# A fused attention and mixture-of-experts layer: the second expert's weight preparation placed behind the last attention output, and the router softmax of the last but one sequence placed at the end of the last sequence's steps

## The chip, the cores and the metric

One core of a Trainium2 chip runs one program. The metric is the device time of the whole program in microseconds (us); lower is better. The engines are PE (TensorE, matmuls), DVE (VectorE), ACT (ScalarE), POOL (GpSimd) and SP (SyncE, which here only starts transfers). Each engine works through its own list of instructions strictly in the order in which the program issues them; engines wait for one another by semaphores.

## What is computed

The input is `x` of 8 sequences, 512 tokens, 256 channels, in float32. The reference, cut to what matters:

```python
k, q, v = proj(W_key), proj(W_query), proj(W_value)      # 16 heads of 16
scores = where(causal, q k^T / sqrt(16), -inf)
out = softmax(scores) v, heads joined, times W_proj^T / 16
x = layernorm(x + out)

s = softmax(x router_w^T, over 8 experts)                # per token
gate_vals, sel_idx = top_k(s transposed, 129)            # per sequence and expert
tokens = x[sel_idx]
y = gelu(tokens @ w1[e] + b1[e]) @ w2[e] + b2[e]         # 256 -> 1024 -> 256
out = zeros.at[sel_idx].add(y * gate_vals)
x = layernorm(x + out)
```

## The kernel before, in words

The kernel has two parts. `attention` (lines 225 to 892) does everything up to the first layernorm, the router's scores and the choice of tokens for the first six sequences. `experts` (lines 1024 to 1453) does the expert layers, the choice for the last two sequences and the second layernorm. In each part every engine has a function that walks through one common list of stages and issues what concerns it.

**The list of attention.** `steps()` (lines 120 to 170) writes this list out. It walks over an index `i`, and for each `i` over 40 places, `place = 10 * g + k`. At a place it yields one score block of sequence `i` (`st`), and the stages that the table `STAGES` (lines 52 to 87) puts at `(g, k)`, each with an offset `ahead` that says which sequence it works on: at index `i` the table's output projection, `rstd`, `logit`, `lexp`, `x1` and `score` stages belong to sequence `i - 1`. There is one more index, `i = B` (8), which only holds the tail of sequence 7. A pair in the code such as `(B, 12)` is an index and a place.

**The stages that matter here.** All line numbers are those of the profile.

- `st`: PE makes a block of scores (L784), ACT takes its exponential (L539), POOL masks it (L468). Two banks `st_ps` are shared in turn, so PE waits for ACT after two blocks.
- `av`: PE multiplies the exponentials by the values (L816), ACT copies the result (L564). `onorm`: PE transposes it (L825), DVE divides (L685, L689). `ot`: PE transposes back (L868), ACT copies (L596). `proj`: four output tiles by PE (L877), and for each of them three DVE instructions (L694, L696, L699); after the fourth DVE writes the variance (L704, L707). The fourth `proj` of sequence 7, at `(B, 21)`, is the last output of attention.
- `rstd`: POOL makes the reciprocal deviation (L497 to L499). `logit`: DVE makes the router's logits (L618, L621, L623). `lexp`: ACT takes the exponential of the logits (L527) and so has to wait for L623. `score`: DVE makes the shares of the softmax (L627, L628, L629) and has to wait for L527. `x1`: ACT finishes a tile of rows (L521); SP stores the rows (L371).
- `pick`, `round`, `picked`, `joined`, `fetch`: the choice of tokens for sequences 0 to 5. DVE runs 17 rounds, each of a maximum of eight, its indices and a replacement (L181, L182, L184); they stand at places 11 to 37 of index 7 (`ROUND_AT`, line 109). After the last one DVE writes `best_f` (L727). At `(B, 3)` PE transposes the result (L207), DVE copies it (L729, L730), PE mirrors one half (L889), DVE joins the halves (L737 to L753), and POOL gathers the tokens of the first two jobs (L513). All `av` blocks of the last group of heads stand behind this on PE, at `(B, 4)` to `(B, 7)`.
- `cut` and `low`: every expert weight is split into a rounded high part and a low part, the rest. The high part is a copy by ACT into the type fp32r; the low part is a subtraction. For expert 0 this is `cut 0` (ACT L553, POOL L505) inside index 7. For expert 1, `load` at `(B - 1, 39)` makes SP fetch both weights (L427, L429); `cut 1` is two copies by ACT of 128x2048 each (L558), for `w1` at `(B, 1)` and for `w2` at `(B, 12)`; `low` at `(B, 11)` is four subtractions by DVE of 128x512 each (L714), for `w1` alone. Those of `w2` belong to `experts` (L1316).

**The start of experts.** The list there is `expert_steps()` (lines 964 to 1005). It begins with `turn` of job 0 and `lastlog`:

```python
yield "turn", 0, 0
yield "lastlog", 0, 0
```

`turn` has PE transpose the gathered tokens (L1389), ACT copy the high part (L1217) and DVE subtract for the low part (L1273). `lastlog` is the `logit`, `lexp` and `score` of sequence 7. Then come the `up` stages: PE (L1416) begins the first one only when both parts of the tokens are there,

```python
if n == 0:
    pe.wait_ge(tp_hi, KC * (q + 1))
    pe.wait_ge(tp_lo, KC * (q + 1))
    pe.wait_ge(w1_cut, PIECES * (e + 1))
```

and ACT then applies Gelu (L1226), for which it loads another table, and copies the high part (L1231); POOL (jobs 0 and 1) subtracts (L1187). `down` (L1434) multiplies by `w2`. SP loads `w1` of expert 2 (L1120) once the low part of expert 1's `w1` is done.

Of the kernel before, what the change touches and what calls it, by code (L numbers as in the profile page):

```python
# [15 lines left out]
B, T, C = 8, 512, 256  # L16
# [87 lines left out]
ROUNDS = -(-CAP // 8)  # L104
PIECES = 4
CUT_AT = [(B - 1, 12 + 3 * piece) for piece in range(2 * PIECES)]
NEXT_CUT_AT, NEXT_LOW_AT = ((B, 1), (B, 12)), (B, 11)
PICK_AT = ((B - 2, 33), (B - 2, 35), (B, 3))
ROUND_AT = [(B - 1, place) for place in (11, 12, 14, 15, 17, 18, 20, 21, 23, 24, 26, 27, 29, 31, 33, 35, 37)]

# [9 lines left out]
def steps():  # L120

    for i in range(-3, B + 1):
        for g in range(4):
            nat_b, nat_0 = (4 * i + g + NAT_LEAD) // 4, (4 * i + g + NAT_LEAD) % 4 * N_QUARTER
            for k in range(10):
                if (i, g, k) == (-1, 3, 0):
                    yield "nmcut", 0, 0
                    yield "v", 1, 2
                    yield "v", 1, 3
                    yield "nm", 0, 0  # L130
                if 0 <= i < B:
                    yield "st", i, (2 * g) * UP + k
                if 0 <= nat_b < B:
                    for n in range(N_QUARTER * k // 10, N_QUARTER * (k + 1) // 10):
                        yield "nat", nat_b, nat_0 + n
                group = i * GROUPS + g - 1
                if k in AV_PLACES and 0 <= group < B * GROUPS:
                    yield "av", group, AV_PLACES.index(k)
                if (i, g, k) == (-2, 0, 0):
                    for stage, n in (("qk", 0), ("qk", 1), ("stack", 0), ("centre", 0), ("qk", 2), ("qk", 3), ("v", 0), ("v", 1), ("v", 2), ("v", 3)):  # L140
                        yield stage, 0, n
                if (i, g, k) == (-1, 2, 0):
                    yield "fold", 0, 0
                for gg, kk, stage, ahead, n in STAGES:
                    if (gg, kk) == (g, k) and 0 <= i + ahead < B and (i, stage, n) not in STARTED:
                        yield stage, i + ahead, n
                for gg, kk, stage, n in SECOND_AT:
                    if i == -1 and (gg, kk) == (g, k):
                        yield stage, 1, n
                        if (stage, n) == ("qk", 1):  # L150
                            yield "stack", 1, 0
                place = 10 * g + k
                if (i, place) == PICK_AT[0]:
                    yield "halved", 0, 0
                if (i, place) == PICK_AT[1]:
                    yield "pick", 0, 0
                if (i, place) in ROUND_AT:
                    yield "round", 0, ROUND_AT.index((i, place))
                if (i, place) in CUT_AT:
                    yield "cut", 0, CUT_AT.index((i, place))  # L160
                if (i, place) == (B - 1, 39):
                    yield "load", 1, 0
                if (i, place) in NEXT_CUT_AT:
                    yield "cut", 1, NEXT_CUT_AT.index((i, place))
                if (i, place) == NEXT_LOW_AT:
                    yield "low", 1, 0
                if (i, place) == PICK_AT[2]:
                    yield "picked", 0, 0
                    yield "joined", 0, 0
                    yield "fetch", 0, 0  # L170


def numbers(stages):

    return {x: n for n, x in enumerate(x for x in steps() if x[0] in stages)}
# [49 lines left out]
def attention(nc, block, both, ctx, xt_d, x_d, wqkv_d, wp_d, wpn_d, rw_d, x1_d, acc_d, ident, mirror, halves, scores, chosen, w1_d, w2_d, b1_d, ahead):  # L225
# [127 lines left out]


    banked = [x for x in steps() if x[0] in BY_ACT + BY_DVE]
    turn_no = {x: n for n, x in enumerate(banked)}

# [9 lines left out]
    def _(sp):  # L367
# [12 lines left out]
        load_xt(0)  # L380
        sp.dma_start(rw[:, :, :], rw_d.rearrange("(k p) n -> p k n", p=P)).then_inc(rw_in, 16)
        for stage, b, n in steps():
            if stage == "split" and b + 1 < B:
                sp.wait_ge(x_split, b + 1)
# [1140 lines left out]
```

## Time and profile before

| what | value |
|---|---|
| time, three runs | 892.38, 891.51, 891.24 us; median 891.51 us |
| profiled execution | 894.26 us, of which the span of all instructions 892.5 us |
| PE busy | 821.0 us, 92% of the span |
| DVE busy | 606.6 us, 68% |
| ACT busy | 532.7 us, 60% |
| POOL busy | 468.0 us, 52% |
| mean granted clock of PE | 0.979 |
| share of the last chain | PE 72%, DVE 14%, ACT 6% |

All times of rows are counted from the start of the span. A timeline row gives the start, the duration, the engine, the line, the operation and the tiles, and in brackets how long the engine stood idle before it and which instruction ended that wait. A row with "x4" merges four instructions in a row. "issue" as a releaser means that the profile shows no instruction that the engine waited for. A granted clock of 1.00 is 2.4 GHz, one of 0.50 is 1.2 GHz. Attention ends and the experts begin at about 460 us.

### The profile page before, as it was taken

The page shows a single profiled execution, that of the slowest core. Times are in us where ns is not written, and L with a number is a line of the kernel's source. Part 1 is how long each engine was busy: PE and PEld are TensorE (multiplying, and loading weights), DVE is VectorE, ACT ScalarE, POOL GpSimd, SP SyncE. Part 2 cuts the span into 40 slices and gives each one's busy share as a digit, 9 for nine tenths or more (in the row PEclk, how much of TensorE's full clock was granted, in tenths as well). Part 3 has the DMA queues.
Part 4 walks back from the last instruction along what each step waited for, and adds up shares of the span by engine and source line. Part 5 has one row for each costly group of instructions (what it writes and reads, how often), then busy time and mean ns, then how long its engine had stood idle before and what let it go on. Part 6 is the DMA issues. An engine that isn't in the chain of part 4 may idle for free.

```text
span 892.5 us, 17252 instructions
## 1 busy us (share of the span) xinstructions
PE 821.0 (92%) x5908; PEld 615.5 (69%) x5908; DVE 606.6 (68%) x2067; ACT 532.7 (60%) x1048; POOL 468.0 (52%) x640
## 2 busy tenths in 40 slices
PE   4779999999999999998778999999999999999994
PEld 3534454454645454433258999999999999999993
DVE  5668777788788778899858854546464554646466
ACT  2247767667586766666647445555565656555546
POOL 6458565666655565344658356445444444545343
PEclk9779999999999999999899999999999999999998
DMA  4863434536352424610253223335243342613275
GB/s 144 221 191 112 133 107 151 155 107 185 123 149 95 159 91 156 192 64 11 89 199 109 30 44 60 91 83 145 40 103 69 53 129 40 150 28 52 31 208 188
DMA packets 89574, 100.12 MB, mean 112 GB/s; under 512 B 8592, under 2 KB 82960, under 8 KB 89360
## 3 DMA queue, kind: packets, MB, share of 16 engines
q1 hardware_dynamic: 72128, 77.66, 27.8%
q0 software_dynamic: 12368, 16.52, 11.4%
q10 hardware_dynamic: 4992, 4.85, 1.8%
q8 instruction: 47, 0.77, 0.4%
q14 instruction: 39, 0.32, 0.1%
HBM read 65.38 MB, written 33.23 MB: 110 GB/s over the span
## 4 chain that ended last, share of the span: by engine, by line
PE 72%; DVE 14%; ACT 6%; issue 3%; POOL 1%; DMA 1%; SPq 1%; ACTq 1%; DVEq 0%; POOLq 0%
PE y_ps L1434 22%; PE h_ps L1416 18%; PE av_ps L816 7%; PE st_ps L784 5%; DVE n_ps L648 5%; PE n_ps L799 5%; PE stage_ps L835 3%; PE stage_ps L877 3%; PE stage_ps L843 3%; PE tp_ps L1389 2%; ACT pt L539 1%; DVE nmax L648 1%; DVE best_at L182 1%; DVE row_pool L184 1%; DVE nm L680 1%
## 5 line engine op out<-in xcount | busy, mean ns | idle before, releaser
L648 DVE CUSTOM_DVE_ANT_0 n_ps<-n_ps,tri 128x512 f32<-128x512 f32 (+3 forms) x512 | 238.6, 519 | 72.5 <-PE n_ps L799 70.5
L539 ACT ACTIVATE pt<-st_ps 128x512 f32<-128x512 f32 x320 | 184.4, 602 | 60.5 <-PE st_ps L784 45.5
L1434 PE MATMUL y_ps<-w_parts,h_hi 128*128 128x256 f32 (+1 forms) x1152 | 215.8, 281 | 2.0 <-POOL h_lo L1187 1.6
L1226 ACT ACTIVATE g<-h_ps,b 128x384 f32<-128x384 f32 (+1 forms) x192 | 104.1, 542 | 164.8 <-PE h_ps L1416 138.4
L1434 PEld LDWEIGHTS y_ps<-w_parts,h_hi 128*128 128x128 f32 (+1 forms) x1152 | 172.6, 177 | 5.9 <-issue 1.9
L1416 PE MATMUL h_ps<-tt_hi,w_parts 128*128 128x384 f32 (+1 forms) x768 | 169.7, 323 | 3.7 <-issue 2.0
L1198 POOL DMA_INDIRECT acc<-y,tok_no x61 | 98.1, 1608 | 140.7 <-DVE y L1342 132.7
L1326 DVE TENSOR_TENSOR h_lo<-g,h_hi 128x384 fp32r<-128x384 f32 (+1 forms) x176 | 90.1, 513 | 115.4 <-ACT h_hi L1231 95.6
L468 POOL TENSOR_SCALAR_AFFINE_SELECT pt<-pt 128x256 f32<-128x256 f32 (+1 forms) x320 | 109.8, 361 | 105.4 <-ACT pt L539 104.6
L1434 PE MATMUL y_ps<-w_parts,h_lo 128*128 128x256 f32 (+1 forms) x576 | 161.5, 280 | 0.0
L784 PE MATMUL st_ps<-w_parts 99*128 99x512 bf16 (+3 forms) x512 | 125.7, 307 | 17.5 <-ACT pt L539 15.9
L799 PE MATMUL n_ps<-w_parts 96*128 96x512 bf16 (+3 forms) x512 | 124.1, 307 | 7.4 <-DVE nmax L648 5.0
L1416 PEld LDWEIGHTS h_ps<-tt_hi,w_parts 128*128 128x128 f32 x768 | 125.4, 188 | 4.7 <-issue 2.2
L1434 PEld LDWEIGHTS y_ps<-w_parts,h_lo 128*128 128x128 f32 (+1 forms) x576 | 102.0, 177 | 2.1
L784 PEld LDWEIGHTS st_ps<-w_parts 99*128 99x128 bf16 x512 | 41.6, 98 | 88.6 <-ACT pt L539 60.5
L1231 ACT ACTIVATE h_hi<-g 128x384 fp32r<-128x384 f32 (+1 forms) x192 | 94.4, 492 | 7.4
L816 PE MATMUL av_ps<-pt,vaug 128*32 128x512 f32 (+3 forms) x1024 | 95.6, 447 | 0.0
L1416 PE MATMUL h_ps<-tt_lo,w_parts 128*128 128x384 f32 (+1 forms) x384 | 91.3, 319 | 0.0
L1169 POOL DMA_INDIRECT tok<-x,tok_no x58 | 57.9, 999 | 33.9 <-issue 33.9
L648 DVE DVE_READ_ACCUMULATOR2_ANT nmax<- 128x1 f32 x512 | 72.3, 141 | 0.0
L799 PEld LDWEIGHTS n_ps<-w_parts 96*128 96x128 bf16 x512 | 43.9, 98 | 36.5 <-DVE nmax L648 22.7
L1416 PEld LDWEIGHTS h_ps<-tt_lo,w_parts 128*128 128x128 f32 x384 | 66.2, 188 | 0.0
(209 smaller groups left out, 1091.0 us busy)
## 6 DMA issues: line engine op xcount, KB each, us to landing
w_parts<-part_d SPq DMA_DIRECT2D x186, 128.0 KB, 2.8
w_raw<-in_w SPq DMA_DIRECT2D x16, 1024.0 KB
part_d<-w_raw SPq DMA_DIRECT2D x96, 128.0 KB, 2.2
w_raw<-in_xt SPq DMA_DIRECT2D x8, 512.0 KB, 4.2
res<-in_x SPq DMA_DIRECT2D x8, 512.0 KB, 4.7
x<-res SPq DMA_DIRECT2D x8, 512.0 KB, 3.3
acc<-res SPq DMA_DIRECT2D x8, 512.0 KB, 5.1
fin<-acc SPq DMA_DIRECT2D x4, 512.0 KB, 4.5
```

The source lines that it names most:

```text
L468: nc.gpsimd.affine_select(out=x, in_=x, compare_op=ALU.is_ge, fill=0.0, base=0, pattern=[[0, len(tiles)], [1, P]], channel_multiplier=-1). ...
L539: nc.scalar.activation(pt[:, slot % PT_RING, n % UP, :], st_ps[at % ST_RING][:, :], ACT.Exp, scale=S_SCALE).then_inc(exp_done, 1)
L648: ins = nc.vector.tensor_tensor_reduce(out=src[:, h, :], in0=src[:, h, :], in1=mask, scale=-1.0, scalar=-BIG_NEG, op0=ALU.add, op1=ALU.min ...
L784: ins = nc.tensor.matmul(st_ps[at % ST_RING][:, c:c + T - kb * P], kst[0:KM, b % 2, h, kb * P:(kb + 1) * P], qst[0:KM, b % 2, h, kb * P:T] ...
L799: ins = nc.tensor.matmul(bank[:, j * w:(j + 1) * w], qst[0:KQ, b % 2, h, qb * P:(qb + 1) * P], kst[0:KQ, b % 2, h, 0:w], start=True, stop= ...
L816: ins = nc.tensor.matmul(av_ps[VW * j:VW * (j + 1), n * P:T], vaug[:, seq % 3, n, h, :], pt[:, (seq * PAIRS + h // 2) % PT_RING, u, c:c + ...
L1198: nc.gpsimd.indirect_dma_start(acc_d[0:reach(j), :], bass.IndirectOffsetOnAxis(ap=choice(e, j), axis=0), y[0:rows_of(j), j, :], None, comp ...
L1226: nc.scalar.activation(g[:, at % G_RING, 0:cols], h_ps[at % H_RING][:, 0:cols], ACT.Gelu, bias=b1[:, e, n:n + 1]).then_inc(g_done, 1)
L1231: nc.scalar.activation(h_hi[:, q % 2, n, 0:cols], g[:, at % G_RING, 0:cols], ACT.Copy).then_inc(g_hi, 1)
L1326: nc.vector.tensor_tensor(h_lo[:, q % 2, n, 0:cols], g[:, at % G_RING, 0:cols], h_hi[:, q % 2, n, 0:cols].bitcast(F32), ALU.subtract).then ...
L1416: ins = nc.tensor.matmul(h_ps[at % H_RING][:, 0:cols], w[e % 2][:, k, units], x[:, q % TOK_RING, k, 0:cols], start=i == 0, stop=i == len(t ...
L1434: ins = nc.tensor.matmul(y_ps[at % Y_RING][0:rows, 0:C], x[:, q % 2, m, toks], w[e % 2][:, m, :], start=i == 0, stop=i == len(terms) - 1)
```

## The change

Three stages move in the list of attention; nothing is added or taken away. The two copies (L558) go from `(B, 1)` and `(B, 12)` to `(B, 24)` and `(B, 25)`, and the four subtractions (L714) from `(B, 11)` to `(B, 26)`, behind the last `proj` and `rstd` of sequence 7. At index 7 alone, that is for sequence 6, `lexp` goes from place 29 to place 38, and `score` from place 32 to place 39.

```diff
@@ -104,7 +104,8 @@
 ROUNDS = -(-CAP // 8)
 PIECES = 4
 CUT_AT = [(B - 1, 12 + 3 * piece) for piece in range(2 * PIECES)]
-NEXT_CUT_AT, NEXT_LOW_AT = ((B, 1), (B, 12)), (B, 11)
+NEXT_CUT_AT, NEXT_LOW_AT = ((B, 24), (B, 25)), (B, 26)
+SCORE_AT = {'lexp': (3, 8), 'score': (3, 9)}
 PICK_AT = ((B - 2, 33), (B - 2, 35), (B, 3))
 ROUND_AT = [(B - 1, place) for place in (11, 12, 14, 15, 17, 18, 20, 21, 23, 24, 26, 27, 29, 31, 33, 35, 37)]
 
@@ -142,6 +143,8 @@
                 if (i, g, k) == (-1, 2, 0):
                     yield "fold", 0, 0
                 for gg, kk, stage, ahead, n in STAGES:
+                    if i == B - 1:
+                        gg, kk = SCORE_AT.get(stage, (gg, kk))
                     if (gg, kk) == (g, k) and 0 <= i + ahead < B and (i, stage, n) not in STARTED:
                         yield stage, i + ahead, n
                 for gg, kk, stage, n in SECOND_AT:
```

## Rows read from the trace of the kernel before

**Rows 1.** Timeline of ACT and PE around the router's exponential of sequence 6.
```profile
431.38 1.08 ACT L539 ACTIVATE pt<-st_ps 128x512 f32<-128x512 f32 x2
435.17 0.23 ACT L527 ACTIVATE lge<-lg 128x32 f32<-128x32 f32 x1 [2.70 <-DVE lg L623]
...
436.42 0.61 PE L784 MATMUL st_ps<-w_parts 99*128 99x256 bf16 x2 [3.51 <-ACT pt L539]
```

**Rows 2.** Groups of DVE from 413.03 to 445.05 us: count, busy us, mean ns, idle.
```profile
L182 DVE FIND_INDEX8 best_at<-best,row_pool 112x8 uint32<-112x256 f32 x17 | 7.1, 419 | 0.0
```

**Rows 3.** Timeline of DVE: shares, what follows them, end of the rounds, next wait.
```profile
439.59 0.19 DVE L627 TENSOR_REDUCE lsum<-lge 128x4 f32<-128x32 f32 x1
...
440.13 0.25 DVE L685 RECIPROCAL rden<-stage_ps 128x16 f32<-128x16 f32 x1
...
444.77 0.27 DVE L727 CAST best_f<-best_at 112x136 f32<-112x136 uint32 x1
446.18 0.42 DVE L729 COPY sides<-stage_ps 128x256 f32<-128x256 f32 x1 [1.14 <-PE stage_ps L207]
```

**Rows 4.** Timeline of PE: the first transpose of the choice, the last outputs.
```profile
445.19 0.29 PE L207 MATMUL stage_ps<-ident,best_f 112*128 112x112 f32 x1 [0.26 <-DVE best_f L727]
...
454.73 5.50 PE L877 MATMUL stage_ps<-wp,o_t 128*128 128x264 f32 x16 [0.83 <-ACT o_t L596]
```

**Rows 5.** Timeline of ACT from its first weight copy to the experts' first tokens.
```profile
447.88 1.91 ACT L558 ACTIVATE w_parts<-w_raw 128x2048 fp32r<-128x2048 f32 x1 [1.93 <-issue]
450.39 0.60 ACT L564 ACTIVATE av_sb<-av_ps 128x512 f32<-128x512 f32 x1 [0.60 <-PE av_ps L816]
450.89 1.90 ACT L558 ACTIVATE w_parts<-w_raw 128x2048 fp32r<-128x2048 f32 x1
453.50 1.08 ACT L596 ACTIVATE o_t<-stage_ps 128x512 f32<-128x512 f32 x2 [0.71 <-PE stage_ps L868]
460.60 0.87 ACT L1217 ACTIVATE tt_hi<-tp_ps 128x384 fp32r<-128x384 f32 x2 [6.01 <-PE tp_ps L1389]
```

**Rows 6.** Timeline of DVE: the four subtractions and what follows them.
```profile
452.61 2.53 DVE L714 TENSOR_TENSOR w_parts<-w_raw,w_parts 128x512 fp32r<-128x512 f32 x4
456.71 0.42 DVE L694 SCALAR_TENSOR_TENSOR res<-stage_ps,res 128x256 f32<-128x256 f32 x1 [1.57 <-PE stage_ps L877]
```

**Rows 7.** Timelines of DVE, POOL, PE and ACT where the experts begin.
```profile
461.70 0.17 DVE L707 TENSOR_SCALAR ve<-mv 128x4 f32<-128x4 f32 x1
461.78 1.01 DVE L1273 TENSOR_TENSOR tt_lo<-tp_ps,tt_hi 128x384 fp32r<-128x384 f32 x2
...
463.66 0.19 DVE L623 TENSOR_TENSOR lg<-lg,rstd 128x32 f32<-128x32 f32 x1 [0.55 <-POOL shift L499]
...
461.96 1.04 POOL L497 TENSOR_TENSOR rstd<-ve,half 128x4 f32<-128x4 f32 x1 [5.35 <-DVE ve L707]
...
460.07 0.82 PE L1389 MATMUL tp_ps<-ident,tok 128*128 128x128 f32 x6
462.90 0.58 PE L1416 MATMUL h_ps<-tt_hi,w_parts 128*128 128x384 f32 x2 [2.01 <-issue]
...
464.26 1.28 ACT L1226 ACT_TABLE_LOAD   x1
465.55 0.58 ACT L1226 ACTIVATE g<-h_ps,b 128x384 f32<-128x384 f32 x1
```

**Rows 8.** Timeline of PE: end of the first unit, a wait, first `down`.
```profile
463.67 0.86 PE L1416 MATMUL h_ps<-tt_hi,w_parts 128*128 128x384 f32 x4
...
473.02 0.62 PE L1416 MATMUL h_ps<-tt_hi,w_parts 128*128 128x384 f32 x2 [1.67 <-ACT g L1226]
...
479.09 0.36 PE L1434 MATMUL y_ps<-w_parts,h_hi 128*128 128x256 f32 x1 [1.60 <-POOL h_lo L1187]
```

**Rows 9.** Windows: length, busy us (count) of PE, PEld, DVE, ACT, POOL, granted clock, DMA.
```profile
435.00:440.00 5.00, 2.69 (x13) 1.53 (x17) 4.64 (x18) 4.83 (x11) 2.41 (x5) 0.50 0.00 0
440.00:445.00 5.00, 4.92 (x40) 1.00 (x32) 4.67 (x17) 3.12 (x7) 2.90 (x6) 0.87 0.93 298
...
455.00:460.00 5.00, 5.00 (x16) 3.81 (x16) 2.47 (x10) 0.00 (x0) 1.30 (x2) 0.67 0.25 72
460.00:465.00 5.00, 2.99 (x20) 2.71 (x18) 3.91 (x19) 1.85 (x4) 2.70 (x7) 1.00 0.70 249
```

**Rows 10.** Weight subtractions of DVE by line: shortest, middle and longest ns, starts.
```profile
L714 DVE TENSOR_TENSOR w_parts<-w_raw,w_parts x4: 682/684/725, 452.6 to 454.4; 128x512 fp32r<-128x512 f32 x4
L1316 DVE TENSOR_TENSOR w_parts<-w_raw,w_parts x4: 693/1328/1509, 471.0 to 475.6; 128x512 fp32r<-128x512 f32 x4
```

## The prediction

> **What bounds the kernel now.** I read the page first: PE has 92% of the span, so what counts is where PE stands still, and the change touches only the stretch from about 430 to 480 us. There I read the timelines engine by engine, then the windows for the clock.
>
> The first thing to see is the stall that the moved exponential makes. ACT ends a pair of score exponentials at 432.46, then stands idle for 2.70 us until DVE's logits let the router's exponential run at 435.17, and PE, behind it, stands idle for 3.51 us [rows 1]. It looks like a prize of about 3 us. But DVE in the same stretch never stops: 17 rounds of the choice, with zero idle before their index searches, run from 413.03 to 445.05 [rows 2], and what comes next on PE, the transpose of the choice, waited only for DVE's `best_f` (0.26 us, at 445.19) [rows 3, 4]. So up to 445 DVE is the bound, and an earlier PE only waits longer there.
>
> The second thing is the tail from 445 to 460. It is one chain of short steps through PE, ACT and DVE. The weight preparation stands beside it: the first copy ends at 449.79 and ACT still waits 0.60 us for PE; the second ends at 452.79 and ACT waits 0.71 us [rows 5]. The four subtractions end at 455.14 and DVE then waits 1.57 us for the first output [rows 6]. All six instructions are covered; taking them from here gives nothing.
>
> The third is the start of the experts. DVE goes from the variance (L707) straight to the low part of the tokens (461.78 to 462.79), and PE starts `up` at 462.90, right after it. DVE's logits of sequence 7 wait 0.55 us for POOL and start L623 at 463.66; the exponential, the table load at 464.26 and the first Gelu at 465.55 hang on it [rows 7]. From there to the first `down` at 479.09 ACT and POOL set the pace (PE waits for Gelu and for POOL's subtraction [rows 8]); behind it PE is busy without a break, so what is late at 479 is late at the end.
>
> **The change part by part.**
>
> *Router exponential and shares, sequence 6.* ACT no longer waits at 432.46 and runs up to 435.30 - 432.46 = 2.8 us ahead (435.30 is about when it resumes, L527 taking 0.23 us from 435.17, with overlap) [rows 1]. The row tiles and their store by SP, the two weight loads behind it on SP, and expert 0's last weight pieces on POOL all come as much earlier; none is waited for by the chain. On DVE the shares leave the chain of rounds: 439.59 to 440.13, 0.54 us, so `best_f` comes 0.54 us sooner [rows 3]. Behind the rounds they fall into DVE's idle 1.14 us before L729 [rows 3], which covers them; without that cover they would cost the 0.54 again. PE ended its scores 0.26 us before L207, so it is ready. Gain on the chain: 0.54 us.
>
> *The two copies on ACT.* 1.91 + 1.90 = 3.81 us, now behind the `ot` copies that end at 454.58. ACT is idle for 6.01 us from there until the experts' tokens at 460.60 [rows 5]. They end near 458.4: covered, with 2.2 us to spare. The loads are long there, since the second copy already ran at 450.89. Cost 0.
>
> *The four subtractions on DVE.* They go into the DVE queue between L707 and L1273. Nothing covers them: DVE has no idle there [rows 7]. Behind them wait `tt_lo` and so PE's first `up`, and the logits and so ACT's exponential, table load and Gelu. By the row they take 2.53 us [rows 6]. Lower bound 2.53. Upper bound: the same kind of subtraction took up to 1.51 us instead of 0.69 beside POOL's subtractions [rows 10]; here POOL has one long instruction beside it, the 1.04 us power of `rstd` [rows 7], so at most 1.04 us more. I take 0.5, half of it, since the nearest rows show both.
>
> The Trainium skill (SBUF — State Buffer, Who interferes with whom) says that a DVE instruction with two SBUF inputs and a GpSimd instruction that reads SBUF exclude one another for a whole instruction. By that rule the term would be the whole 1.04 us; by the L714 row alone it would be nothing. `tt_lo`, which ran beside the power without loss, reads one operand from PSUM.
>
> *From DVE to the Gelu.* `tt_lo` and PE's `up` come 2.53 - 0.54 = 1.99 us later. The logits had waited 0.55 us for POOL, which will be done long before. So the exponential and the Gelu come 1.99 - 0.55 = 1.44 us later without contention, 1.94 with it. SP's load of expert 2's `w1` comes as much later and is needed only jobs later. The four row tiles of sequence 7 and POOL's gathers shift along.
>
> *PE's clock.* Before, PE stood idle 2.01 us between the token transposes and `up` and kept a granted clock of 1.00 [rows 7, 9]. Now that gap is 2.01 + 2.53 to 3.03, about 4.8 us. The nearest row is the 3.51 us of idle: behind it the clock was 0.50 from 435 to 440 and, by the 0.87, until 441.3, some 4.8 us after PE resumed at 436.42; the other dip, 455 to 458.3 (0.67 x 5 us), came after scattered short transposes [rows 9]. So I expect half clock for 3.3 to 4.8 us of `up`. At half clock PE loses half that time, 1.7 to 2.4 us. PE leads ACT there: the first unit's last matmuls are in the four that start at 463.67, so it is done by about 464.2, and Gelu started at 465.55 [rows 7, 8], a lead of 1.3 us, which shrinks by 1.99 - 1.44 to 0.8. So ACT is late by 0.9 to 1.6 us more; I take 1.2. Lower bound 0 (clock stays up), upper 2.4 (no lead left).
>
> *Sum.* -0.54 + 2.53 - 0.55 + 0.5 + 1.2 = +3.14, about +3.1 us. It is a difference within the profiled execution (894.26 us, span 892.5 and 1.8 around it), which stands 2.75 us above the median of the three runs. I apply it to the median: 891.5 + 3.1 = 894.6 us.
>
> **The rivals.**
>
> 1. *The plain sum.* The clock holds over the gap and POOL does not get in the way: +1.44 us, 892.9. For it: the 2.01 us gap cost nothing. Against: a gap of more than twice that, and the 3.51 us one was punished.
>
> 2. *The clock also falls in the tail.* With the stall gone PE finishes its scores up to 3 us before `best_f`, and until the last `av` it then has only transposes. Half clock over `av`, transposes and outputs would add to the chain; the 16 output matmuls took 5.50 us with 3.3 us of dip [rows 4, 9], that is about 1.7 us lost per such dip. +3.1 + 1.7 = +4.8, 896.3. Against it: the clock might recover before `av`.
>
> 3. *The clock is better placed in the tail.* PE has no 3.5 us hole at 433, and the dip over the outputs goes away: 1.7 us less on PE, of which DVE's own three instructions per tile leave about 1.0. +1.44 - 1.0 = +0.4, 891.9.
>
> 4. *Faster: the first copy was in the way in the timed runs.* ACT waited 1.93 us for something that the profile does not name, which I read as the landing of expert 1's `w1`; the copy ended 0.60 us before PE's result [rows 5]. If the load lands over 0.60 us later in an unprofiled run, the copy delays ACT's L564, and with it the whole tail; the change takes that away. With a landing 3 us later it would give 2.4 us; with the better clock as well, 1.44 - 2.4 - 1.0 = -2.0, 889.5. It decides against the rest when the landing is more than about 2 us later. The trace has the landing in time, and the three runs lie within 1.2 us, so this is weak.
>
> 5. *The score move does nothing*, if ACT had another wait in the same place: then 0.54 is missing and the result is +3.7, inside the forecast's range.
>
> **How the numbers follow.** Forecast (+2.4 to +4.2, with or without part of contention and clock) 0.50; rival 1, 0.17; rival 2, 0.14; rival 3, 0.09; rival 4, 0.06; others 0.04. A measurement of this kernel tells about 0.2%, 1.8 us, from no change. Slower by more than that: the forecast and rival 2, and the fifth of rival 1 whose contention lifts it over 893.3: 0.67. Within: rest of rival 1, rival 3 and some others, 0.25. Faster: rival 4 and a rest, 0.08. The range leaves out rival 4 and the ends of rival 2: from 891.8, below rival 3, to 897.0, which is rival 2 with the full contention of 1.04 instead of 0.5.
>
> **What would show it.** In the changed profile: L527 for sequence 6 behind the last scores, no 2.7 us idle on ACT at 432; PE waiting up to 3 us for `best_f` before L207; `best_f` near 444.5; the copies between the `ot` copies and L1217; the four L714 directly behind L707, near 461.3 to 464; `up` starting near 465 to 465.4; the first Gelu near 467 to 467.5; the granted clock at 0.50 for part of 464 to 470; the first `down` near 482.3. I am wrong if PE's first `up` is less than 1 us later than 462.90, or if the time is below 891.8: then either the subtractions found cover or the tail gained more than the rounds' 0.54 us.

## The result, and the profile after

The changed kernel takes 897.0 us (median of 6 runs, 895.67 to 900.07) against 891.56 us for the kernel before in the same comparison; the ratio is 1.0064 with a 95% interval of 1.0052 to 1.0077, that is 4.6 to 6.9 us slower. The ratios leave out two executions in a much slower state, one of the kernel before (1307.58 us) and one of `subs_only` below (1562.88 us). The direction was forecast, the size was not: +3.1 us, with a range up to 897.0. The profiled execution is the slowest of the six (900.07 us), as that of the kernel before also stands above its median (894.26 us); its span is 898.3 us against 892.5, so +5.8 us is the difference to be found. Line numbers from 107 on are 1 to 3 higher than before: L816 is now L819, L877 is L880, L1416 is L1419.

PE of the changed kernel, timeline:

```profile
433.38 0.61 PE L787 MATMUL st_ps<-w_parts 99*128 99x256 bf16 x2 [0.58 <-ACT pt L542]
...
445.56 0.29 PE L210 MATMUL stage_ps<-ident,best_f 112*128 112x112 f32 x1 [2.92 <-DVE best_f L730]
...
448.03 4.50 PE L819 MATMUL av_ps<-pt,vaug 128*32 128x512 f32 x32
...
457.19 5.42 PE L880 MATMUL stage_ps<-wp,o_t 128*128 128x264 f32 x16 [0.83 <-ACT o_t L599]
...
467.67 0.98 PE L1419 MATMUL h_ps<-tt_hi,w_parts 128*128 128x384 f32 x2 [4.41 <-issue]
...
484.86 0.36 PE L1437 MATMUL y_ps<-w_parts,h_hi 128*128 128x256 f32 x1 [1.55 <-POOL h_lo L1190]
```

The stall of 3.51 us [rows 1] is gone (0.58 us at 433.38), and PE waits for `best_f` instead, 2.92 us where it had waited 0.26 [rows 4]. Then comes what I had only as a rival: the last `av` block takes 4.50 us. In the kernel before the same 32 matmuls read:

```profile
447.37 2.36 PE L816 MATMUL av_ps<-pt,vaug 128*32 128x512 f32 x32
```

Two DVE rows of the kernel before, to compare with (L621 and L1273 are L624 and L1276 now):

```profile
434.72 0.19 DVE L621 TENSOR_TENSOR lg<-scores,lmax 128x32 f32<-128x32 f32 x1
...
468.13 1.02 DVE L1273 TENSOR_TENSOR tt_lo<-tp_ps,tt_hi 128x384 fp32r<-128x384 f32 x2 [3.04 <-issue]
```

DVE and POOL of the changed kernel, timelines:

```profile
434.59 1.14 DVE L624 TENSOR_TENSOR lg<-scores,lmax 128x32 f32<-128x32 f32 x1
435.76 0.32 DVE L626 TENSOR_TENSOR lg<-lg,rstd 128x32 f32<-128x32 f32 x1
...
445.19 0.23 DVE L730 CAST best_f<-best_at 112x136 f32<-112x136 uint32 x1
...
464.07 0.17 DVE L710 TENSOR_SCALAR ve<-mv 128x4 f32<-128x4 f32 x1
464.15 2.49 DVE L717 TENSOR_TENSOR w_parts<-w_raw,w_parts 128x512 fp32r<-128x512 f32 x4
466.56 1.01 DVE L1276 TENSOR_TENSOR tt_lo<-tp_ps,tt_hi 128x384 fp32r<-128x384 f32 x2
...
434.41 1.26 POOL L508 TENSOR_TENSOR w_parts<-w_raw,w_parts 128x512 fp32r<-128x512 f32 x1 [0.33 <-ACT w_parts L556]
...
464.33 1.41 POOL L500 TENSOR_TENSOR rstd<-ve,half 128x4 f32<-128x4 f32 x1 [7.17 <-DVE ve L710]
```

`best_f` starts 0.42 us later than before (444.77 [rows 3]), not 0.54 us earlier. The reason is L624, a logit subtraction of 128x32, which took 0.19 us before and takes 1.14 here; it starts 0.18 us after a POOL subtraction and ends 0.06 us after that one ends. L626 behind it takes 0.32 us instead of 0.19, so the two cost 1.08 us more; less the 0.54 us of the shares that makes 0.54, of which 0.12 don't show in the 0.42, because the whole stretch lies 0.12 us earlier in this profile (the PE block at 432.04 before starts at 431.92). The four subtractions of the weights cost what their row said, 2.49 us.

ACT of the changed kernel, timeline:

```profile
468.15 0.23 ACT L530 ACTIVATE lge<-lg 128x32 f32<-128x32 f32 x1 [4.31 <-DVE lg L626]
470.01 1.28 ACT L1229 ACT_TABLE_LOAD   x1 [1.63 <-PE h_ps L1419]
471.31 0.58 ACT L1229 ACTIVATE g<-h_ps,b 128x384 f32<-128x384 f32 x1
```

The table load now waits 1.63 us for PE's first unit of `up`. Before, it came 0.14 us behind the exponential's end and 1.36 us behind the start of `up` [rows 7].

Windows of the changed kernel (the third number from the end is the granted clock):

```profile
435.00:440.00 5.00, 5.00 (x24) 1.57 (x23) 4.71 (x15) 3.37 (x7) 3.45 (x7) 0.51 0.55 184
440.00:445.00 5.00, 2.63 (x27) 0.75 (x23) 4.67 (x17) 2.77 (x6) 1.67 (x5) 1.00 1.01 309
445.00:450.00 5.00, 3.60 (x22) 1.78 (x26) 3.21 (x18) 0.00 (x0) 0.33 (x1) 0.68 0.40 136
450.00:455.00 5.00, 4.08 (x32) 2.05 (x24) 1.39 (x5) 0.60 (x1) 3.78 (x5) 0.64 0.28 79
455.00:460.00 5.00, 3.88 (x15) 3.08 (x16) 0.82 (x4) 4.04 (x4) 1.85 (x2) 0.70 0.29 82
460.00:465.00 5.00, 3.26 (x17) 2.47 (x15) 4.17 (x17) 1.51 (x3) 0.67 (x1) 0.96 0.24 66
465.00:470.00 5.00, 2.33 (x7) 2.36 (x8) 3.96 (x13) 0.23 (x1) 4.06 (x9) 0.73 0.79 279
```

The clock is down four times: from 435 to 440, over the `av` block, over the outputs and over the first unit of `up`. The first and the third are there before as well [rows 9]. The first is there although the stall of 3.51 us ahead of it is gone.

How late each landmark is, after minus before, from these rows and those of before:

| landmark | before | after | late by |
|---|---|---|---|
| `best_f` starts | 444.77 | 445.19 | 0.42 |
| last `av` block starts | 447.37 | 448.03 | 0.66 |
| outputs start | 454.73 | 457.19 | 2.46 |
| variance | 461.70 | 464.07 | 2.37 |
| first `up` | 462.90 | 467.67 | 4.77 |
| first Gelu | 465.55 | 471.31 | 5.76 |
| first `down` | 479.09 | 484.86 | 5.77 |

The span's 5.8 us is complete at the first `down`: about 2.4 us before the variance, 2.4 us of subtractions, 1.0 us between `up` and Gelu. One part of this comparison stays open: from the end of the `av` block to the first output it is 5.00 us in the profile before, 4.66 in this one and 4.23 to 4.26 in all twelve others of the study. No run tells why.

### The profile page after: what moved, and what is told of

Same layout as the page of the kernel before. It is cut to its first block, busy times and chain, and to the rows that moved or that the text cites. A ratio compares the mean times of both kernels' runs of the same rounds, so it can differ in the third digit from the quotient of the medians.

```text
span 898.3 us, 17251 instructions
## 1 busy us (share of the span) xinstructions
PE 827.3 (92%) x5908; PEld 620.5 (69%) x5908; DVE 605.6 (67%) x2067; ACT 532.3 (59%) x1048; POOL 468.8 (52%) x640
## 4 chain that ended last, share of the span: by engine, by line
PE 72%; DVE 14%; ACT 6%; issue 3%; POOL 2%; DMA 2%; ACTq 1%; SPq 0%; DVEq 0%; POOLq 0%
PE y_ps L1437 22%; PE h_ps L1419 18%; PE av_ps L819 7%; PE st_ps L787 5%; PE n_ps L802 5%; DVE n_ps L651 5%; PE stage_ps L838 4%; PE stage_ps L846 3%; PE stage_ps L880 3%; PE tp_ps L1392 2%; ACT pt L542 1%; DVE nmax L651 1%; DVE best_at L185 1%; DVE row_pool L187 1%; PE stage_ps L871 1%
## 5 line engine op out<-in xcount | busy, mean ns | idle before, releaser
L1419 PE MATMUL h_ps<-tt_hi,w_parts 128*128 128x384 f32 (+1 forms) x768 | 170.8, 324 | 5.7 <-issue 4.4
L1419 PEld LDWEIGHTS h_ps<-tt_hi,w_parts 128*128 128x128 f32 x768 | 126.2, 189 | 6.7 <-issue 4.6
L819 PE MATMUL av_ps<-pt,vaug 128*32 128x512 f32 (+3 forms) x1024 | 98.2, 459 | 0.0
L1419 PE MATMUL h_ps<-tt_lo,w_parts 128*128 128x384 f32 (+1 forms) x384 | 91.8, 320 | 0.0
L1419 PEld LDWEIGHTS h_ps<-tt_lo,w_parts 128*128 128x128 f32 x384 | 66.8, 189 | 0.0
```

Of the source, the lines that this page charges most:

```text
L819: ins = nc.tensor.matmul(av_ps[VW * j:VW * (j + 1), n * P:T], vaug[:, seq % 3, n, h, :], pt[:, (seq * PAIRS + h // 2) % PT_RING, u, c:c + ...
L1419: ins = nc.tensor.matmul(h_ps[at % H_RING][:, 0:cols], w[e % 2][:, k, units], x[:, q % TOK_RING, k, 0:cols], start=i == 0, stop=i == len(t ...
```

## The experiments

### The parts apart

Four kernels in one comparison, each timed against the kernel before (median 891.86).

**score_only**: `lexp` and `score` moved, weight work at its old places.

```diff
-NEXT_CUT_AT, NEXT_LOW_AT = ((B, 24), (B, 25)), (B, 26)
+NEXT_CUT_AT, NEXT_LOW_AT = ((B, 1), (B, 12)), (B, 11)
```

> Only the router's exponential and shares of sequence 6 are moved; the weight copies and subtractions stay where they were before. Theory A (the score move costs by PE's clock and by one blocked DVE instruction): in the profile after, the choice's last rounds ended 0.4 us later, not 0.54 us earlier, since the logits' L624 ran 1.14 us beside a POOL subtraction, and the last av block took 4.50 us at half clock instead of 2.36; together the first output matmul came 2.5 us later. So this kernel alone should be about 2 to 2.5 us slower than before, near 893.8, and its granted clock between 447 and 453 us should be at 0.50. Rival B (my prediction: the score move gains 0.54 us and all the loss is in the weight subtractions): 891.0, best_f ending near 444.5.

Measured: 894.31 us, ratio 1.0026 (1.0018 to 1.0035), so 2.3 us slower. Its DVE and PE timelines:

```profile
433.55 1.14 DVE L624 TENSOR_TENSOR lg<-scores,lmax 128x32 f32<-128x32 f32 x1
...
444.52 0.42 PE L210 MATMUL stage_ps<-ident,best_f 112*128 112x112 f32 x1 [2.45 <-DVE best_f L730]
...
447.75 3.55 PE L819 MATMUL av_ps<-pt,vaug 128*32 128x512 f32 x32
```

Both marks are there: L624 at 1.14 us and a slow `av` block. The move that I had booked as a gain is a loss.

**weights_only**: copies and subtractions moved, router stages at their old places (`SCORE_AT = {}`).

> Only the two copies and the four subtractions are moved; the router's exponential and shares stay. Theory A: the four subtractions put 2.5 us between the variance and the tokens' low part, PE's first up starts 2.5 us later (near 465.4), and it may come back at half clock, up to 1 us more on the first Gelu: +2.5 to +3.5 us, 894.0 to 895.0. Av block at about 2.4 us. Rival B (the parts only hurt together): within 1 us of before.

Measured: 895.27 us, ratio 1.0037 (1.0024 to 1.0050), 3.3 us slower.

```profile
447.92 2.36 PE L819 MATMUL av_ps<-pt,vaug 128*32 128x512 f32 x32
...
463.40 0.58 PE L1419 MATMUL h_ps<-tt_hi,w_parts 128*128 128x384 f32 x2 [4.41 <-issue]
...
465.20 1.28 ACT L1229 ACT_TABLE_LOAD   x1 [1.09 <-PE h_ps L1419]
```

The `av` block is at full speed, and the gap ahead of `up` is 4.41 us instead of 2.01. The two parts add: 2.3 + 3.3 = 5.6 us, the whole change 5.7 by its ratio. The prediction's terms for this part were 2.53 - 0.55 + 0.5 + 1.2 = 3.7 us.

**subs_only**: as weights_only, but the copies stay at `(B, 1)` and `(B, 12)`.

> Only the four DVE subtractions are moved behind the last output; the two ACT copies stay at their old places and the router's stages too. Theory A: the copies are free in both places, so this is the same as weights_only within 0.4 us (894.0 to 895.0). Rival B: the copies behind the ot copies cost something of their own (ACT busy 3.7 us ahead of the experts' tokens), then this is faster than weights_only by 1 us or more.

Measured: 894.98 us, ratio 1.0030 (1.0018 to 1.0041). The intervals of the two overlap widely: no cost or gain of the copies is seen in either place, as forecast.

**subs_after_logits**: as weights_only, with the subtractions issued behind the logits and shares of sequence 7 (the stage `low` of attention is left out).

```diff
                 for ins in take_halves(nc, halves, scores, slice(EARLY, B)):
                     ins.then_inc(halved, 1)
+                dve.wait_ge(w1_top, 2 * PIECES)
+                for piece in range(PIECES):
+                    nc.vector.tensor_tensor(piece_of(w1_lo[1], "w1", piece), piece_of(w1_raw, "w1", piece),
+                                            piece_of(w1_hi[1], "w1", piece).bitcast(F32), ALU.subtract).then_inc(w1_cut, 1)
```

> As weights_only, but the four subtractions are issued in the experts' part behind the logits, shares and halves of sequence 7, where DVE stood idle 3.04 us before the second job's tokens. Theory A (what costs is only the place in front of the tokens' low part and the logits): the 2.5 us disappear into that idle time, up starts near 462.9 and the time is 891.5 within 0.6. Rival B (the work on DVE is what costs, wherever it stands in the experts' part): 893.5 to 894.5. Rival C: the subtractions now run beside POOL's subtractions, take 1.1 to 1.5 us each instead of 0.6 and push the second job's tokens: +1 to +2.

Measured: 891.57 us, ratio 0.9993 (0.9984 to 1.0001), no difference from before. Its DVE timeline:

```profile
462.68 2.49 DVE L1280 TENSOR_TENSOR w_parts<-w_raw,w_parts 128x512 fp32r<-128x512 f32 x4
465.81 1.02 DVE L1270 TENSOR_TENSOR tt_lo<-tp_ps,tt_hi 128x384 fp32r<-128x384 f32 x2 [0.65 <-ACT tt_hi L1214]
```

The same 2.49 us, a few instructions later, fill what was DVE's wait of 3.04 us for the second job's tokens, and 0.65 us of it is left.

### What makes the score move a loss

**after_tail_fill**: the changed kernel with idle PE time filled ahead of `best_f`.

```diff
             elif stage == "picked":
+                for _ in range(12):
+                    nc.tensor.matmul(ps[:, :], ident_b[:, :], tri[:, :, :].rearrange("p a k -> p (a k)"), start=True, stop=True)
                 pe.wait_ge(best_ready, 1)
```

> The changed kernel with 12 extra matmuls of 128x512 bf16 on PE, issued before it waits for best_f, into the bank that the transposes then overwrite; their results are not used. Theory A (the lower clock over the last av block comes from PE standing idle ahead of best_f): the idle 2.9 us is filled, the clock stays at 1.00 from 446 to 453, the av block takes 2.36 us instead of 4.50, and the time falls by 1.5 to 2 us against the changed kernel, to about 895.2. Rival B (the clock falls whatever PE does there, or what counts is the tail's short steps): av still 3.5 to 4.5 us and 897.0.

Measured: 895.94 us, ratio 1.0041 (1.0029 to 1.0054), about 1.1 us less than the changed kernel by the medians, 2.1 by the ratios; the two intervals just touch, so the size is uncertain.

```profile
443.17 2.75 PE L888 MATMUL stage_ps<-tri,ident_b 128*128 128x512 bf16 x12
...
447.92 2.36 PE L819 MATMUL av_ps<-pt,vaug 128*32 128x512 f32 x32
```

Nothing but PE's idle time was changed, and the `av` block is back at 2.36 us. Over all 14 profiles of the study the block took 2.36 us in the four with the router stages at their old place, 3.55 to 4.50 in the five that move them, and 2.36 in the five that move them and have the extra matmuls. In the five with the longer block PE had stood idle for 2.27 to 3.26 us ahead of `best_f`, in the nine others for 0.53 us at most.

**score_cut6**: score_only with expert 0's last two weight pieces later.

```diff
-CUT_AT = [(B - 1, 12 + 3 * piece) for piece in range(2 * PIECES)]
+CUT_AT = [(B - 1, at) for at in (12, 15, 18, 21, 24, 27, 32, 34)]
```

> As score_only, but expert 0's seventh weight piece (ACT copy and POOL subtraction) stands at place 32 instead of 30, and the eighth at 34, so that POOL isn't subtracting when DVE makes the logits of sequence 6. Theory A (L624's 1.14 us is a wait for POOL's 1.27 us subtraction, as both read two SBUF operands): L624 takes 0.19 us again and best_f ends 0.95 us earlier relative to the rounds before it; the time falls by about 1 us against score_only, to 893.3. Rival B (the 1.14 us belong to the order of DVE's own work): L624 stays at 1.14 us.

Measured: 892.23 us, ratio 1.0002 (0.9993 to 1.0011). DVE, POOL and PE timelines:

```profile
434.47 0.23 DVE L624 TENSOR_TENSOR lg<-scores,lmax 128x32 f32<-128x32 f32 x1
...
444.03 0.23 DVE L730 CAST best_f<-best_at 112x136 f32<-112x136 uint32 x1
...
436.25 1.27 POOL L508 TENSOR_TENSOR w_parts<-w_raw,w_parts 128x512 fp32r<-128x512 f32 x1 [0.61 <-ACT w_parts L556]
...
446.73 3.86 PE L819 MATMUL av_ps<-pt,vaug 128*32 128x512 f32 x32
```

With POOL's subtraction at 436.25 instead of beside it, L624 takes 0.23 us, and `best_f` starts 0.74 us earlier than before; measured from the score blocks at 432.04 (here 431.80) it is 0.50, the forecast 0.54 us. The time fell by more than the 1 us expected (2.1 us by medians and ratios, over two comparisons); the rest is not explained, as the `av` block is still slow in the profile. The eleven runs lie in two groups, 890.7 to 891.4 and 892.2 to 894.0 us; perhaps the block takes longer in some executions only, which a single profile can't show.

**score_cut6_fill**: both remedies together.

> score_cut6 and the 12 extra matmuls ahead of best_f. Theory A (what the score move cost is the blocked L624 and the clock, nothing else): with both taken away my term of -0.54 us is left, so 891.0 to 891.4, and the first transposes of the choice come 0.5 us earlier relative to the start of the rounds than before. Rival B (something else of the score move costs): 892 or more.

Measured: 890.77 us, before 891.89; ratio 0.9994 (0.9984 to 1.0004). With L624 and the clock put right, the score move is no loss. The medians show 1.1 us of gain, the interval does not exclude none. Its profile has one more dip:

```profile
459.86 0.83 PE L1421 MATMUL h_ps<-tt_hi,w_parts 128*128 128x384 f32 x2 [2.00 <-issue]
```

The gap ahead of `up` is that of the kernel before, 2.00 us, and yet the first unit runs at half clock. Behind such a gap the unit kept its full clock in five profiles and lost it in this one; behind 4.41 us it lost it in all five that had this gap.

### Between the tokens and the Gelu

**after_up_fill**: the changed kernel with 20 matmuls of 128x384 into the bank that the first `up` overwrites, ahead of the wait for the tokens.

```diff
+                if q == 0 and n == 0:
+                    pe.wait_ge(w1_cut, PIECES)
+                    for _ in range(20):
+                        nc.tensor.matmul(h_ps[0][:, 0:384], w1_hi[0][:, 0, 0:P], w1_hi[0][:, 1, 0:384], start=True, stop=True)
```

> The changed kernel with 20 extra matmuls of 128x384 on PE between the token transposes and the first up, into the bank that up then overwrites; not used. Theory A (the first unit of up runs at half clock because of the 4.4 us of idle, and ACT's table load waits for that unit): the first unit takes 1.1 us instead of 2.1, the first Gelu comes 1 us earlier against the start of up, and the time is 896.0 to 896.3 instead of 897.0. Rival B (PE has a lead over ACT there, as my prediction had it): under 0.3 us of difference.

Measured: 896.87 us, ratio 1.0051 (1.0038 to 1.0063). The median of 5 runs hardly moved and the ratio fell by 0.0013, 1.2 us; the time does not decide. The trace does, locally:

```profile
461.83 0.17 DVE L710 TENSOR_SCALAR ve<-mv 128x4 f32<-128x4 f32 x1
...
465.43 0.59 PE L1423 MATMUL h_ps<-tt_hi,w_parts 128*128 128x384 f32 x2 [0.92 <-issue]
...
466.80 1.28 ACT L1229 ACT_TABLE_LOAD   x1 [0.67 <-PE h_ps L1423]
468.10 0.58 ACT L1229 ACTIVATE g<-h_ps,b 128x384 f32<-128x384 f32 x1
```

From the start of `up` to the table load it is 1.37 us here, 470.01 - 467.67 = 2.34 in the changed kernel, 1.36 before [rows 7]. It is also 1.36 us in score_only, subs_after_logits, score_cut6 and best_try, with the exponential ending 0.13 to 0.14 us ahead of the load. Where the load needn't wait for PE (after_preload, below) it follows the exponential by 0.01 us. So it was already PE's unit, and not the exponential, that released the load in the kernel before, by a small margin.

From the variance to the first Gelu it is 468.10 - 461.83 = 6.27 us here, 3.85 before [rows 7]: 2.42 us more, which is the delay of `up`, and nothing of the logits' 0.55 us comes off.

**after_preload**: the changed kernel with a one-column Gelu behind the router's exponential.

```diff
                 seen["exponentials"](B - 1)
+                act.wait_ge(ahead["b1_in"], 16)
+                nc.scalar.activation(g[:, 2, 0:1], b1[:, 0, 0:1], ACT.Gelu)
```

> The changed kernel with a Gelu of one column on ACT right behind the router's exponential of sequence 7, so that the Gelu table is loaded then and not after the wait for the first unit of up; its result is not used. Theory A (the 1.28 us table load stands behind the wait for PE's first unit in the changed kernel, where ACT waited 1.63 us for it): the load falls into that wait and the first Gelu starts about 0.3 us after the unit's last matmul, 1.2 us earlier; time 895.8 instead of 897.0. Rival B (the load is started ahead of the wait anyway, as in the kernel before where it began at 464.26 right behind the exponential): no difference.

Measured: 896.78 us, ratio 1.0061 (1.0049 to 1.0073): no difference that can be seen, against the 1.2 us expected.

```profile
466.13 1.28 ACT L1246 ACT_TABLE_LOAD   x1
467.43 0.20 ACT L1246 ACTIVATE g<-b 128x1 f32<-128x1 f32 x1
467.54 0.56 ACT L1229 ACTIVATE g<-h_ps,b 128x384 f32<-128x384 f32 x1
468.13 0.52 ACT L1234 ACTIVATE h_hi<-g 128x384 fp32r<-128x384 f32 x1
469.09 0.58 ACT L1229 ACTIVATE g<-h_ps,b 128x384 f32<-128x384 f32 x1 [0.44 <-PE h_ps L1421]
```

The load did move ahead of the wait for PE, and the first Gelu followed 2.13 us after the start of `up` (465.41) instead of 3.64. But then the second Gelu waits for PE, still at half clock: part of the saving is handed back one unit later. From `up` to the first `down` it is 16.33 us here and 17.19 in the changed kernel, so 0.86 us in the profile; in the times it was not found.

**after_plain_sum**: the changed kernel, subtractions at their new place, with all four remedies (the later weight pieces, both sets of extra matmuls, the early table load).

> The changed kernel, subtractions at their new place, with everything else that I hold to cost taken away: the seventh weight piece later (L624 free of POOL), 12 extra matmuls ahead of best_f, 20 ahead of the first up, the Gelu table loaded early. Theory A: what is left is the plain sum of the DVE terms, -0.54 + 2.5 - 0.55 = +1.4 us against before, near 893.2, and less the part of PE's dips that this kernel also avoids, so 892.3 to 893.5. Rival B (a further cost that I have not found): 894.5 or more.

Measured: 892.93 us, ratio 1.0018 (1.0010 to 1.0027), 1.3 us over its kernel before (891.66). That is close to the plain DVE sum of the prediction, +1.4 us. The profile bears both terms out: `best_f` comes 12.22 us after the score blocks instead of 12.73, and from the variance to the Gelu it is 1.88 us more than before. But the second figure needs the early table load, which takes PE's unit out of the chain; the changed kernel does not have it. And the extra matmuls may also take away dips that the kernel before has, which no run separates.

### Versions that might beat both

**best_try** is the changed kernel with the subtractions behind the logits (as subs_after_logits), the later weight pieces and the 12 matmuls.

> The changed kernel with the subtractions moved on behind the logits and shares of sequence 7, the seventh weight piece later, and 12 extra matmuls ahead of best_f. Theory A: the gain of the shares (0.54 us) and no cost: 890.8 to 891.2 against 891.9 of before, at least as fast as score_cut6_fill. Rival B (the two good parts collide, as by subtractions beside POOL): 892 or more.

Measured: 891.73 us, ratio 1.0000 (0.9992 to 1.0009). Its one profiled execution has a span of 887.6 us, the lowest seen, but the median of 11 runs is that of the kernel before: a single profile proves little here.

**best_try_up** is best_try with 9 matmuls ahead of `up` and the early table load.

> best_try with 9 extra matmuls ahead of the first up and the early table load. Theory A (in some runs the clock falls over the 2.0 us ahead of up and costs up to 1 us, as in the profile of score_cut6_fill): the median falls by 0.2 to 0.6 us against best_try and the spread is smaller. Rival B (the dip is rare, or the extra matmuls delay the tokens' transposes): equal or slower.

Measured: 890.91 us, ratio 0.9992 (0.9983 to 1.0001). The lowest ratio of the study, 0.7 us under the kernel before, and not certain to be below it. Nothing tried here beats the kernel before beyond the error.

## Why the prediction was wrong

The direction and the cost of the subtractions stood; the size was too small by 2.3 us. The score move was off by 2.8 us: -0.54 forecast, +2.3 measured (score_only). The weight part was 3.7 us by the prediction's terms and 3.3 in weights_only, partly by luck, as shown below.

**The step that failed: "Gain on the chain: 0.54 us".** The score move costs 2.3 us alone (score_only). Two things took the gain's place. First, DVE's list was taken as fixed in its durations. With ACT 2.8 us ahead, POOL's subtraction of weight piece 7 landed on the logits, and L624 and L626 together took 1.08 us more; moving the piece away gives it back (score_cut6). The prediction had these pieces "come as much earlier; none is waited for by the chain": true of the semaphores, not of the time they take beside DVE. I had looked for such a clash only at the new place of the subtractions. Second, the idle time that PE no longer spent at 433, where DVE covered it, it spent ahead of `best_f`, and the clock fell over the `av` block, which is on the chain: 4.50 - 2.36 = 2.14 us in this profile, 1.19 us in that of score_only. This was rival 2. Its mechanism is shown by after_tail_fill; its price (1.7 us) was near, its chance (0.14) far too low: in all five profiles that had the move and no extra matmuls the block was slow. The sentence "an earlier PE only waits longer there" named the cause and priced it at nothing.

**The subtractions.** 2.53 us forecast, 2.49 measured, `up` 2.40 us later against the variance; covered by nothing, as said. They would have been free a few instructions later (subs_after_logits), a cover that the prediction's own rows did not show but the 3 us wait of DVE did.

**Contention at the new place, 0.5 us: none.** The Trainium skill (SBUF — State Buffer, Who interferes with whom) says that a DVE instruction with two SBUF inputs and a GpSimd instruction that reads SBUF exclude one another. The traces agree in part. At 434.6 DVE's L624 ended with POOL's subtraction. At the new place it was POOL's power that got longer (1.41 us instead of 1.04 [rows 7]) and DVE kept its time: the power spans parts of three subtractions, which took 0.68 to 0.69 us each as before [rows 10], so an exclusion for whole instructions is not what this row shows. In both places the instruction that started second was the one that paid.

**The logits' wait for POOL, -0.55 us: the wait is gone, the gain is not there.** The prediction let the table load and the Gelu hang on the exponential; they hung on PE's first unit of `up`, already before (1.36 us from the start of `up` to the load, see after_up_fill). So the Gelu came later by all that `up` did, 2.42 us at full clock and not 1.9. This error of 0.55 us and the 0.5 us of contention that did not come cancel: that is the luck in the weight part.

**PE's clock over `up`, +1.2 us: size about right, reasoning wrong.** I gave PE a lead of 1.3 us over ACT, up to the Gelu at 465.55. The table load, 1.28 of these 1.3 us, stands behind the wait for PE's unit, so the lead was nothing. The half clock cost 1.0 us from `up` to Gelu. The row on which the dip was forecast, the 3.51 us stall that "was punished", does not show it either: with that stall cut to 0.58 us the clock was 0.51 from 435 to 440 all the same. What shows it here are the five profiles with 4.41 us ahead of `up`, and after_up_fill, which fills the gap and has the full clock.

**The plain sum** of the DVE terms without contention, +1.44 us, is near what after_plain_sum measured, +1.3. It says what the DVE terms are worth once PE's unit is out of the way of the table load; it isn't the changed kernel without its dips.

**Rivals 1, 3, 4 and 5.** The clock did not hold over the gap in the changed kernel (1). The outputs kept their dip in its profile (3). The first copy was not in the way: taking the copies away from there gained nothing beyond the error (weights_only against subs_only) (4). Rival 5 had another wait of ACT in the same place: there was none, PE's wait for ACT fell from 3.51 to 0.58 us.

## What to carry to other kernels

Removing a stall that another engine covers does not remove the idle time, it moves it; ask where PE will be idle next and whether what follows there is on the chain, since it may then run at half clock. When an engine is released to run ahead, every instruction of its neighbours is shifted against the others: look at what comes to lie beside a short instruction on the bounding engine. Work that one engine must do once belongs behind the instructions that others wait for, even if only by a few places.

## What the runs showed of the hardware

- A short DVE subtraction of two SBUF operands (128x32, 0.19 us) took 1.14 us when it started 0.18 us after a POOL subtraction of 1.26 us. It took 0.19 to 0.23 us in every profile where POOL's was elsewhere.
- Unused matmuls in idle time kept the clock up: with 2.75 us of them ahead of `best_f` the block behind the transposes took 2.36 us in five profiles, without them 3.55 to 4.50 us in five.
- The dip over the 16 output matmuls varies between executions: 5.4 to 5.5 us in three of the 14 profiles (before, changed, after_tail_fill), 3.82 us in the other eleven. The changed kernel (5.42 us) and after_up_fill and after_preload (3.82 us) issue the same instructions up to there. So two profiles can differ by 1.6 us in this stretch with no difference in the program ahead of it; what decides is not known.
- An activation table load stands behind the semaphore wait of the activation that needs it. A dummy activation moved it ahead: it began at 466.13, 0.01 us behind the exponential, instead of after a wait of 1.63 us for PE.
